# Gate carried in scattered rows, expert rows added onto the residual tile by DMA, ring of five jobs

## The reference, cut to what matters

```python
    top_p, top_i = jax.lax.top_k(probs, TOP_K)            # two experts of each token, and their gates
    cap = int(np.ceil(T * TOP_K / E * CAP_FACTOR))        # 1280 rows for each expert
    ...
    buf = buf.at[exp_idx, pos_c].add(ln2[tok] * keep[:, None].astype(dtype))
    h1 = jax.nn.gelu(jnp.einsum('ech,efh->ecf', buf, moe_w1))
    h2 = jnp.einsum('ecf,ehf->ech', h1, moe_w2)
    out_ent = h2[exp_idx, pos_c] * (gate * keep.astype(dtype))[:, None]
    moe_out = jnp.zeros((T, H_), dtype).at[tok].add(out_ent)
    return hidden_after_attn + moe_out.reshape(S_, B_, H_)
...
x = x + s * g                                             # g = silu of the FFN's result
```

## Time and profile before

| | us |
|---|---|
| median of 3 runs | 2144.31 |
| lowest and highest run | 2137.54, 2151.8 |
| profiled execution, its span | 2142.5 |
| PE busy | 1864.6 (87%) |
| DVE busy | 1398.3 (65%) |
| POOL busy | 911.2 (43%) |
| ACT busy | 822.7 (38%) |

### The profile page before, as it was taken

How to read it: one execution, slowest core, us unless ns; L and a number is a source line. 1 busy time by engine, 2 the same in 40 slices (tenths; PEclk the granted TensorE clock), 3 DMA queues, 4 the chain that set the end, 5 groups by cost and what they waited for, 6 DMA issues and landing times. The chain is left out here.

```text
span 2142.5 us, 37546 instructions
## 1 busy us (share of the span) xinstructions
PE 1864.6 (87%) x13095; PEld 1661.7 (78%) x13096; DVE 1398.3 (65%) x3479; ACT 822.7 (38%) x1945; POOL 911.2 (43%) x1399
## 2 busy tenths in 40 slices
PE   2688888729899998997899999999787898878998
PEld 1476767628599885997899999999664798855997
DVE  2566666365456554554678878887476688785787
ACT  1455555316333373332233333333254233452332
POOL 4345454216545465452413322331174356570554
PEclk7799999859999999999899999999898999998999
DMA  4243433111301112011344334333243122241122
GB/s 133 103 153 119 152 117 117 59 37 57 118 31 53 60 58 96 28 47 45 126 127 129 119 109 128 119 117 100 78 122 117 30 75 85 89 147 50 50 63 72
DMA packets 152646, 194.77 MB, mean 91 GB/s; under 512 B 19849, under 2 KB 137935, under 8 KB 150430
## 3 DMA queue, kind: packets, MB, share of 16 engines
q1 hardware_dynamic: 109486, 122.16, 18.4%
q0 software_dynamic: 16928, 49.43, 7.3%
q10 hardware_dynamic: 26064, 20.99, 2.9%
HBM read 105.24 MB, written 88.21 MB: 90 GB/s over the span
## 5 line engine op out<-in xcount | busy, mean ns | idle before, releaser
L1719 ACT ACTIVATE hid<-bank 128x512 f32<-128x512 f32 x160 | 95.7, 598 | 330.3 <-PE bank L128 325.5
L126 PE MATMUL bank<-rows_hi,up_hi 128*128 128x256 f32 x640 | 188.5, 295 | 7.0 <-POOL up_lo L1785 7.0
L128 PE MATMUL bank<-rows_hi,up_lo 128*128 128x256 f32 x640 | 181.8, 284 | 0.0
L127 PE MATMUL bank<-rows_lo,up_hi 128*128 128x256 f32 x640 | 181.7, 284 | 0.0
L128 PE MATMUL bank<-down_hi,hid_lo 128*128 128x256 f32 x640 | 181.2, 283 | 0.0
L126 PE MATMUL bank<-down_hi,hid_hi 128*128 128x256 f32 x640 | 181.1, 283 | 0.0
L127 PE MATMUL bank<-down_lo,hid_hi 128*128 128x256 f32 x640 | 181.1, 283 | 0.0
L1822 DVE TENSOR_TENSOR hid_lo<-hid,hid_hi 128x512 fp32r<-128x512 f32 x160 | 140.7, 894 | 54.8 <-ACT hid_hi L1719 53.5
L1109 POOL DMA_INDIRECT buf_d<-lt,to_row x128 | 130.4, 1019 | 79.8 <-issue 24.8
L1423 PE MATMUL bank<-wconv,knt 128*128 128x128 f32 x1280 | 156.4, 278 | 0.0
L1119 POOL DMA_INDIRECT job_picked<-h_d,from_row x128 | 133.4, 1042 | 52.6 <-issue 22.4
(11 more groups left out here) (302 smaller groups left out, 5647.6 us busy)
## 6 DMA issues: line engine op xcount, KB each, us to landing
buf_d<-zeros SPq DMA_DIRECT2D x16, 1280.0 KB, 7.5
rows_in<-buf_d SPq DMA_DIRECT2D x80, 256.0 KB, 3.0
h_d<-h ACTq DMA_DIRECT2D x80, 256.0 KB, 3.5
x<-in_x SPq DMA_DIRECT2D x16, 512.0 KB, 5.1
after_d<-after SPq DMA_DIRECT2D x16, 512.0 KB, 2.9
ln_d<-ln SPq DMA_DIRECT2D x16, 512.0 KB, 3.2
xa<-in_x SPq DMA_DIRECT2D x16, 512.0 KB, 4.2
lt<-ln_d SPq DMA_DIRECT2D x64, 128.0 KB, 2.0
```

Source lines behind the costliest of these rows:

```text
L126: pe.matmul(dst, hi, mhi, start=start and i == 0, stop=False)
L127: pe.matmul(dst, hi, mlo, start=False, stop=False)
L128: mm = pe.matmul(dst, lo, mhi, start=False, stop=end)
L1719: act.activation(dst[:, 2 * half:2 * half + 2].rearrange("p f c -> p (f c)"), bank[half][:], ACT.Gelu_apprx_tanh).then_inc(e_hid, 1)
```

## The change

The rows in `buf_d` become 272 instead of 256 elements wide (`ROW = E + 16`): 1088 bytes, of which column 256 holds the gate of that token for that expert. The tile `lt` holds a token's row twice, once for each expert, so SP loads it twice; POOL copies the two gates into it before the scatter and sets the columns behind them to zero once. In the experts `result_out` multiplies by that column instead of copying, so `h2_d` holds weighed rows. For that the chunk's rows stay until `result_out` is done: the ring becomes four, released by `h2_made`.

In the second call `mix` goes away. SP loads the residual straight into the tile `mixed`; POOL gathers the first expert's rows onto it with an indirect DMA that adds, and one step later, once that has landed, the second expert's. ACT takes the tanh of `mixed` into a tile of its own (ring of two). The ring of jobs becomes five, that of `s` stays three, with its loads issued apart (`load_s`). `add_first` comes one step after the job's number, `add_second` two steps after, where `pick` came three steps after. Semaphores of the set-up are cleared by POOL in the routing part and used again.

```diff
-        buf_d = nc.dram_tensor("buf_d", (SLOTS, E), F32).ap()
+        buf_d = nc.dram_tensor("buf_d", (SLOTS, ROW), F32).ap()
...
             with nc.Block() as block:
+                @block.gpsimd
+                def _(pool):
+                    for done_with in passing_sems:
+                        pool.sem_clear(done_with)
...
-        SCATTERS, RING = TILES // 2, 3
+        SCATTERS, RING, S_RING, TANH_RING = TILES // 2, 5, 3, 2
...
-                            sp.dma_start(lt[p][:], tile(ln2_d, job)).then_inc(lt_in[p], 16)
+                            for k in range(2):
+                                sp.dma_start(lt[p][:, k, 0:E], tile(ln2_d, job)).then_inc(lt_in[p], 16)
...
                             if job >= RING:
                                 sp.wait_ge(job_made, job - RING + 1)
+                            sp.dma_start(mixed[p][:], tile(after_d, t)).then_inc(after_in[p], 16)
+                            if job >= RING:
                                 sp.wait_ge(job_out[p], 16 * (rounds(job) - 1))
-                            for dst, src in ((job_after, after_d), (job_x, a["x"])):
-                                sp.dma_start(dst[p][:], tile(src, t)).then_inc(job_in[p], 16)
+                            sp.dma_start(job_x[p][:], tile(a["x"], t)).then_inc(job_x_in[p], 16)
+
+                        def load_s(job):
                             if not is_own(job):
-                                sp.dma_start(job_s[p][:], tile(s_d, t)).then_inc(job_s_in[p], 16)
+                                p = job % S_RING
+                                if job >= S_RING:
+                                    sp.wait_ge(job_made, job - S_RING + 1)
+                                sp.dma_start(job_s[p][:], tile(s_d, batch_tile(job))).then_inc(job_s_in[p], 16)
...
                         def scatter(job):
                             p = job % 2
-                            pool.wait_ge(lt_in[p], 16 * rounds(job))
+                            if job < 2:
+                                pool.memset(lt[p][:, :, E:ROW], 0.0).then_inc(lt_gated, 1)
+                                pool.wait_ge(lt_gated, 2 * job + 1)
+                            if job >= 2:
+                                pool.wait_ge(scattered[p], 32 * (rounds(job) - 1))
+                            pool.tensor_copy(lt[p][:, :, E], gate[:, job]).then_inc(lt_gated, 1)
+                            pool.wait_ge(lt_gated, job + 1 + min(job + 1, 2))
+                            pool.wait_ge(lt_in[p], 32 * rounds(job))
...
-                        def pick(job):
+                        def add_first(job):
                             p = job % RING
-                            if job >= RING:
-                                pool.wait_ge(job_made, job - RING + 1)
-                            for k in range(2):
-                                rows = bass.IndirectOffsetOnAxis(from_row[:, batch_tile(job), k:k + 1], axis=0)
-                                pool.indirect_dma_start(picked[p][:, k], None, h2_d, rows).then_inc(picked_in[p], 16)
+                            pool.wait_ge(after_in[p], 16 * rounds(job))
+                            rows = bass.IndirectOffsetOnAxis(from_row[:, batch_tile(job), 0:1], axis=0)
+                            pool.indirect_dma_start(mixed[p][:], None, h2_d, rows, compute_op=ALU.add).then_inc(picked_in[p], 16)
+
+                        def add_second(job):
+                            p = job % RING
+                            pool.wait_ge(picked_in[p], 32 * rounds(job) - 16)
+                            rows = bass.IndirectOffsetOnAxis(from_row[:, batch_tile(job), 1:2], axis=0)
+                            pool.indirect_dma_start(mixed[p][:], None, h2_d, rows, compute_op=ALU.add).then_inc(picked_in[p], 16)
...
-                            if not scatters and 0 <= i - LATE < BT:
-                                pick(job_of(b, i - LATE))
+                            if not scatters and 0 <= i - 2 < BT:
+                                add_second(job_of(b, i - 2))
+                            if not scatters and 0 <= i - 1 < BT:
+                                add_first(job_of(b, i - 1))
...
-                            if not scatters and 0 <= k - 2 < BT:
-                                pick(own(b, k - 2))
+                            if not scatters and 0 <= k - 1 < BT:
+                                add_second(own(b, k - 1))
+                            if not scatters and 0 <= k < BT:
+                                add_first(own(b, k))
...
-                            act.wait_ge(job_mixed, job + 1)
-                            act.activation(picked[job % RING][:, 1], picked[job % RING][:, 0], ACT.Tanh, scale=0.5).then_inc(job_silu, 1)
+                            p = job % RING
+                            act.wait_ge(picked_in[p], 32 * rounds(job))
+                            if job >= TANH_RING:
+                                act.wait_ge(job_made, job - TANH_RING + 1)
+                            act.activation(job_tanh[job % TANH_RING][:], mixed[p][:], ACT.Tanh, scale=0.5).then_inc(job_silu, 1)
...
+            ROWS_AHEAD = 4
-            rows_in = [sb(f"rows_in{p}", [P, 2, E], F32, own) for p in range(2)]
+            rows_in = [sb(f"rows_in{p}", [P, 2, ROW], F32, own) for p in range(ROWS_AHEAD)]
...
-                        if i >= 2:
-                            sp.wait_ge(rows_turned, i - 1)
-                        sp.dma_start(rows_in[i % 2][:], chunk_of(buf_d, i)).then_inc(rows_loaded[i % 2], 16)
+                        p = i % ROWS_AHEAD
+                        if i >= ROWS_AHEAD:
+                            sp.wait_ge(h2_made, i - ROWS_AHEAD + 1)
+                        sp.dma_start(rows_in[p][:], chunk_of(buf_d, i)).then_inc(rows_loaded[p], 16)
...
-                        dve.tensor_copy(h2[i % 2][:].rearrange("p r e -> p (r e)"), bank[4 + i % 2][:]).then_inc(h2_made, 1)
+                        dve.tensor_tensor(h2[i % 2][:], bank[4 + i % 2][:].rearrange("p (r e) -> p r e", e=E),
+                                          rows_in[i % ROWS_AHEAD][:, :, E:E + 1].to_broadcast((P, 2, E)), ALU.mult).then_inc(h2_made, 1)
```

More of the change, by code:

```diff
@@ L41 @@
 SLOTS = NX * CAP
+ROW = E + 16
 FAR = 1 << 20
@@ L853, in build @@
         front_only.close()
+        setup_only.close()
         ax_in = [sem("ax_in0"), sem("ax_in1")]
@@ L947, in attend @@
                 if scatters:
-                    lt = [mine(f"lt{p}", [P, E]) for p in range(2)]
+                    lt = [mine(f"lt{p}", [P, 2, ROW]) for p in range(2)]
                 else:
-                    picked = [mine(f"job_picked{p}", [P, 2, E]) for p in range(RING)]
-                    job_after, job_s, job_x = ([mine(f"job_{w}{p}", [P, E]) for p in range(RING)] for w in ("after", "s", "x"))
+                    mixed, job_x = ([mine(f"job_{w}{p}", [P, E]) for p in range(RING)] for w in ("mixed", "x"))
+                    job_s = [mine(f"job_s{p}", [P, E]) for p in range(S_RING)]
+                    job_tanh = [mine(f"job_tanh{p}", [P, E]) for p in range(TANH_RING)]
                 soon = range(BT // 2) if scatters else range(BT)
@@ L976, in s_loads @@
                 def s_loads(job):
-                    return len([j for j in range(job % RING, job + 1, RING) if not is_own(j)])
+                    return len([j for j in range(job % S_RING, job + 1, S_RING) if not is_own(j)])
                 def tile(ap, t):
@@ L1070, in _ @@
                                 load_job(job)
+                                if job < S_RING:
+                                    load_s(job)
                             load_x(first, 2)
@@ L1075, in _ @@
                                     load_job(job + RING)
+                                if job + S_RING < 2 * EACH:
+                                    load_s(job + S_RING)
                                 if job == 0:
@@ L1533, in first_loop @@
                                 job = job_of(b, j)
-                                dve.wait_ge(job_s_in[job % RING], 16 * s_loads(job))
-                                join(job, job_s[job % RING])
-                            if not scatters and 0 <= j + 1 < BT:
-                                mix(job_of(b, j + 1))
+                                dve.wait_ge(job_s_in[job % S_RING], 16 * s_loads(job))
+                                join(job, job_s[job % S_RING])
                         def plus_one(b, g):
@@ L1648, in second_loop @@
                                     dve.tensor_tensor(lo[:, f], gel[:, f % 4], hi[:, f], ALU.subtract).then_inc(gel_split, 1)
-                                if not scatters:
-                                    mix(own(b, k - 1))
-                                    mix(own(b, k))
                             k = i - 6
```

66 lines of the change are left out of this document (30 added, 36 removed).

## The result

The changed kernel takes 2289.75 us in the median (2275.74 to 2326.0, 4 runs) against 2142.7 (2137.54 to 2151.8, 4 runs) for the kernel before: a ratio of 1.0654, 95% interval 1.0604 to 1.0704. It is slower by 6.5%. The ratio leaves out the run of 2326.0 us, whose granted clock was 0.861 where the other three had 0.928 to 0.938. The forecast, 2156, was wrong, and so was its range. The profiled execution has a span of 2273.8 us; before it was 2142.5, so 131.3 us are to be explained.

What follows compares the result with a forecast made beforehand. PE was taken to bound the experts, with DVE and POOL both close to the limit in the second attention stage. Terms -24 + 34 + 3 = +13 on 2142.5 gave 2155.5, say 2156 us; range 2118 to 2205.

Steps and rivals of the forecast that it cites:

- experts: Experts stage: row loads land late behind the next weights, PE stalls 2.4 us 13 times; with smaller items +34 us.
- second stage, first loops: Second attention stage: steps of 5.1 us, 15.6 us a batch over no jobs instead of 17; -3 us.
- tails: Ends of both first loops in the second attention stage: 15.3 us each against 23.70 and 24.90; -18 us.
- second loops: Second attention stage: 3 of the remaining 4 us that jobs cost credited as saved; -3 us.
- scatters: First attention stage: gate copies on POOL, second load, wider rows, mostly covered by POOL's room; +3 us.
- load shares: Rival, experts: row load moves beside the weights, lands in 4.0 us, stall 1.2 us; 2140 us, chance 0.15.
- load not late: Rival, experts: row load lands in 3.0 us, the stage loses only 3 us; 2124 us, chance 0.07.
- DVE was the only bound: Rival, second attention stage: POOL's wait hides, first loops fall back to those without jobs; 2121 us, chance 0.12.
- I take 5.2: Experts: assumed landing of a row load just behind weights, 5.2 us, between 3.0 and 6.0.
- L: Second attention stage: time from a job's first adding gather's issue to its landing, taken as 3.7 us, between 3.1 and 5.1.
- the 1.4: Second attention stage: the second gather's issue and gap, about 1.4 us, added to the first's landing for a 5.1 us step.
- slow adding: Rival, second attention stage: adding gather lands in 5.1 us, step 6.5 us, loops lose 32 us; 2196 us, chance 0.24.

Runs made afterwards that it cites:

- ring6: Changed kernel with six row-tile buffers instead of four in the experts, so row loads go two chunks earlier: 2209.27 us, ratio 1.0292.
- no_add: ring6 with both gathers of a job overwriting instead of adding, order and waits unchanged: span 2147.7 us, second attention stage 610.8 us.
- late_second: ring6 with the second adding gather of a job one step later in the second attention stage: span 2179.0 us.
- one_lt: ring6 with scattered rows loaded once and no gate copied or waited for: first attention stage 557.9 us against 562.0.
- before_ring4: Kernel before, with four pairs of gathered tiles instead of three and gathers issued one step earlier: 2133.48 us, ratio 0.9947.
- plain_ring4: ring6 with two plain gathers per job, DVE adding both rows and the residual, ring of four: 2142.07 us, ratio 0.9981.
- no_weights: Changed kernel, row ring still four, loading weights only for the first two experts: experts 524.6 us.

## Why the prediction was wrong, point by point

| term | forecast | measured | what gave it |
|---|---|---|---|
| experts | +34 | +75.0 | ring6: -74 with two more row tiles |
| second stage, first loops | -3 | +20.7 | no_add, late_second |
| tails | -18 | +14.1 | no_add: 23.9, 24.9 |
| second loops | -3 | +15.2 | no_add: as before; in part open |
| scatters | +3 | +6.3 | open: one_lt is within the spread |

The middles and the end of the second attention stage, which have no term of their own, are 2.2 us shorter.

**Right.** The stage split and its readings held. PE idles behind late row loads, fifteen times, in the place named and fourteen times behind the weights named. DVE lost its waits for picked rows. POOL waits ahead of `add_second` for the first landing. The estimate of that landing, 3.7 us, was close to the 3.9 measured, and the rivals "load shares", "load not late" and "DVE was the only bound" did not happen.

**The experts, mis-sized by more than half.** Two steps failed. "I take 5.2" for the landing of a row load behind weights: it was 6.1 to 7.1 in eleven of fifteen. The upper bound of 6.0 came from a store and from a row load 1.2 us behind its weights; the new load is only 0.8 us behind. Fifteen stalls came to 48.2 us, 3.2 each, where 2.4 stood in the sum thirteen times. And the sum ended with the stall. It has no term for the stretch behind it, where the clock is low: twelve chunks took 1.3 to 2.5 us longer than 6.2, in all 23 us. 48 + 23 is 71 of the 75. The three other stalls, of 0.6, 1.3 and 2.4 us, have a chunk of 6.25 us behind them: stalls of the length that the prediction gave them might have had no such stretch at all. The earlier trace rows had a hint: where PE hardly waits, the experts' clock is 0.98, and in the first loop with its gaps it is 0.87 and 0.84.

**The step of the second stage: not L, but the 1.4.** The prediction said that a step can't be shorter than L "plus the second's issue and gap, about 1.4 us". The form was right: in the step shown, 3.75 to the landing + 0.74 from there to the second's issue + 1.68 for this issue + 0.31 = 6.48. The 1.4 was 2.7. Some 0.6 of the 1.3 us that were missing is issue, priced by plain gathers ("POOL's 4.8 us stay"); the other 0.7 is gap, above all the 0.74 us between the landing and the next issue (0.74 in the median of such waits, too). Loops and tails of both batches were forecast at 188.6 us in all (91.2, 66.8 and twice 15.3) and took 244.3. Of the 55.7 us too many, fifteen steps in each of two batches give about 40 by issue and gap, and only 6 by the 0.2 us in L; the other 10 are not traced. no_add has 202.4: without the adding, 14 us too many would have been left. The rival "slow adding", for which I gave the landing alone as the deciding number, comes out on the right side (slower) by luck, since the mechanism is another: POOL's time, not the DMA's. The bounds, 3.1 and 5.1, held for the landing and said nothing of issue; the range had no place for it. Two slips are small beside this: ten steps in 57.0 us are 5.7, not 5.6, and the sum of "slow adding" leaves out the two x norms that the forecast's has, 7 us in all.

**The tails.** The prediction counted fifteen steps in the loop and one in the tail. The trace has four in the tail: in batch 3's, L1147 is issued at 2033.13, 2039.81, 2046.30 and 2053.17, since PE's tiles run ahead of POOL's norms. So some of the long steps are paid in the tail, where 18 us were to be saved. no_add has four there too, at some 5.6 us, and tails of 23.9 and 24.9: the count was wrong whatever a gather costs. That the tail of before was set by gathered rows that come late was wrong as well: with a ring of four and the gathers one step earlier (before_ring4) it stayed at 23 to 24 us, though DVE waits only 0.2 us for gathered rows in batch 3's.

**The second loops.** I credited 3 us for DVE's relief. They lost 15, and no_add has them at 169.8 and 166.8, near those of before. That POOL's longer issues delay `cnorm` there, as they delay `qnorm` in the first loop, is only argued: in batch 2's second loop ACT waits 33.7 us for it against 30.3 before and 30.4 in no_add, but 33.9 in plain_ring4 too, which has that loop at 176.8 without adding.

**The scatters.** 3 us stood for what took 6.3. The cover named was POOL's room in a first loop; the first loops lost 0.7 and 0.9 us, their tails 0.7 each and the second loops 3.4 and 3.9, while the middles are 2 us shorter each. Of the second loops I had read no row. What the 6.3 us are stays open: plain_ring4 has the same scatters at 3 us over the kernel before, as forecast, and no_weights at 10.

## What to carry to other kernels

Price an operation moved onto a DMA by the issuing engine's time as well as by its landing, above all on an engine that is in order and near its limit: here DVE gave 57 us of busy time away, POOL took 72, and the stage grew by 48. When a buffer's release moves to a later point, look for what stands in the DMA queues at the new moment, and count a long stall of TensorE with the low clock behind it. And measure the parts of a change alone: a longer ring with earlier gathers was worth 11 us in the kernel before, and two row buffers more took back 74 in the changed one.

## What the runs showed of the hardware

An indirect DMA that adds took POOL 1.56 and 1.68 us to issue where the same one without adding took 0.97 and 1.10 (medians of no_add), moved its rows in four times the packets, and landed after 3.9 to 4.1 us in place of 3.0 to 3.4.

A row load behind weights has both halves of the argument that the prediction weighed. Queue rows of the changed kernel in 1083.1 to 1086.1, the three microseconds after the load's issue; of the same in 1086.1 to 1090.1, until it landed; and of no_weights in 1084.5 to 1086.0, just after its issue (packets, MB, share of 16 engines; q0 has the weights, q1 the rows, q10 the stores):

```profile
q0 software_dynamic: 197, 0.74, 78.9%
```
```profile
q1 hardware_dynamic: 486, 0.51, 44.6%
q10 hardware_dynamic: 402, 0.39, 27.9%
q0 software_dynamic: 84, 0.28, 19.0%
```
```profile
q1 hardware_dynamic: 31, 0.03, 34.3%
```

Without weights ahead, the rows begin within 1.5 us. Behind weights no packet of theirs moves for 3 us; then they run among the weights and the stores. The Trainium skill (DMA: Bandwidth & Descriptors, "Queues, rings and completion order") has a DMA engine drain a whole packet of one queue, typically some 9 to 17 descriptors, before it turns to the next. The second stretch, in which the queues move side by side, agrees. Whether the first does is not shown: if what the profile counts are descriptors, the 197 of q0 are some 12 on each of 16 engines (an estimate), a wait that the rule allows, and not the sharing from the start that the prediction read out of it.

Behind stalls of TensorE of 0.6, 1.3 and 2.4 us the next chunk took 6.25 us, where 6.2 is usual. Behind the twelve longest of the fifteen stalls, 2.5 to 4.1 us, the next chunk took 1.3 to 2.5 us longer at a lower granted clock (0.71 and 0.68 in the mean of the two chunks shown), though PE was busy throughout.
